# Attention: queries and keys without rotary part projected for two batches at once

## The reference, cut to what matters

```
q = x @ Wq.T ; k = x @ Wk.T ; v = x @ Wv.T
q_nope, k_nope: (B, 256, 16, 128)     q_rope, k_rope: (B, 256, 16, 64), rotated by position
scores = q_nope.k_nope / sqrt(128) + q_rope.k_rope / sqrt(64)
out = softmax(scores) . v ; x = layernorm(x + out @ Wo.T)
```

## Time and profile before

| | us |
|---|---|
| three runs | 673.15, 671.19, 672.73 (median 672.73) |
| the profiled execution | 671.22 |
| its span | 669.4 |
| the 16 slots of the first attention begin at | 22.06 |
| slot 15 begins at | 377.82 |

### The profile page before, as it was taken

The page is one execution under the profiler, slowest core; times in us unless marked ns, Lnnn a source line. Parts: engine busy times, 40 slices in busy tenths (PEclk is TensorE's granted clock), DMA queues, the critical chain, the costliest instruction groups (busy, mean ns, idle before and its releaser), DMA issues. The chain is left out here.

```text
span 669.4 us, 15275 instructions
## 1 busy us (share of the span) xinstructions
PE 656.9 (98%) x5297; PEld 632.3 (94%) x5297; DVE 439.2 (66%) x968; ACT 410.9 (61%) x1085; POOL 246.3 (37%) x279
## 2 busy tenths in 40 slices
PE   8999999999999999999999999999999999999995
PEld 8999999999999999999999899999997799999995
DVE  5566557656665765765675677556569986556877
ACT  5566667566776666766577773334689964333553
POOL 2731863034353133632329555112361462222011
PEclk9999999999999999999999999999999999999998
DMA  7174665435534445534363304100166100000010
GB/s 255 38 220 153 197 172 144 138 98 174 169 124 115 123 124 178 157 122 131 97 194 125 97 2 151 32 0 0 48 200 245 72 1 1 1 1 0 1 33 31
DMA packets 38172, 69.74 MB, mean 104 GB/s; under 512 B 3440, under 2 KB 22640, under 8 KB 37872
## 3 DMA queue, kind: packets, MB, share of 16 engines
q1 hardware_dynamic: 37696, 68.38, 33.6%
q10 hardware_dynamic: 432, 0.79, 0.4%
HBM read 52.18 MB, written 16.97 MB: 103 GB/s over the span
## 5 line engine op out<-in xcount | busy, mean ns | idle before, releaser
L312 PE MATMUL PJ<-xTh,WBh 128*128 128x256 f32 x364 | 106.7, 293 | 0.0
L314 PE MATMUL PJ<-xTh,WBl 128*128 128x256 f32 x364 | 103.0, 283 | 0.0
L313 PE MATMUL PJ<-xTl,WBh 128*128 128x256 f32 x364 | 102.8, 282 | 0.0
L851 POOL TENSOR_TENSOR stage<-stage 128x256 f32<-128x256 f32 x32 | 24.5, 766 | 162.8 <-DVE stage L718 162.8
L611 ACT ACTIVATE probs<-probs,rinv 128x256 f32<-128x256 f32 x128 | 58.4, 508 | 26.7 <-DVE rinv L734 26.7
L1229 PE MATMUL UG<-xTh,WBh 128*128 (+1 forms) x256 | 73.6, 288 | 0.3 <-PEq L54 0.3
L1232 PE MATMUL UG<-xTh,WBl 128*128 (+1 forms) x256 | 72.4, 283 | 0.0
L1230 PE MATMUL UG<-xTl,WBh 128*128 (+1 forms) x256 | 72.4, 283 | 0.0
L1301 ACT ACTIVATE ga<-UG 128x256 f32<-128x256 f32 x64 | 24.5, 383 | 75.5 <-PE UG L1232 75.5
L312 PEld LDWEIGHTS PJ<-xTh,WBh 128*128 128x128 f32 x364 | 69.6, 191 | 0.5
L313 PEld LDWEIGHTS PJ<-xTl,WBh 128*128 128x128 f32 x364 | 69.6, 191 | 0.0
(11 more groups left out here) (326 smaller groups left out, 2364.1 us busy)
## 6 DMA issues: line engine op xcount, KB each, us to landing
K<-scr_k SPq DMA_DIRECT2D x60, 256.0 KB, 4.4
raw<-in_w_att SPq DMA_DIRECT2D x37, 256.0 KB, 4.8
Q<-scr_q SPq DMA_DIRECT2D x15, 512.0 KB, 7.5
stage<-scr_m SPq DMA_DIRECT2D x6, 768.0 KB, 4.4
scr_q<-rot_h SPq DMA_DIRECT2D x30, 128.0 KB
scr_q<-rot_l SPq DMA_DIRECT2D x30, 128.0 KB
scr_k<-rot_h SPq DMA_DIRECT2D x30, 128.0 KB
scr_k<-rot_l SPq DMA_DIRECT2D x30, 128.0 KB
```

Of the source, the lines that this page charges most:

```text
L312: pe.matmul(out, ah, bh, start=(i == 0), stop=False)
L313: pe.matmul(out, ah, bl, start=False, stop=False)
L314: last = pe.matmul(out, al, bh, start=False, stop=(i == n - 1))
```

## The change

Queries and keys without rotary part are projected for a pair of batches: for slots 2 and 3, 4 and 5, and so on, one matmul streams 512 token columns. An odd slot computes heads 0 and 1 (weights at 2) of the next pair, an even slot heads 2 and 3 (weights at 4) of its own pair. `QKh[:, 0]` and `QKl[:, 0]` now hold heads 0 and 1 of both batches, `[:, 1]` heads 2 and 3. Slot 0 projects batch 1 in the old form, and so do the pieces ahead of the slots. The values stay as they were.

The rotary pieces stay in step 2 of even slots and go to step 0 of odd ones, where the other pieces go to steps 1 and 2. ACT takes the rotary parts one step later, as before: now step 1 of an odd slot. On POOL the splits of weights 8 and 9 go behind the rotations, and the split of the feed-forward weights waits for scores of slot 15. PSUM banks and waits follow the new order.

```diff
-        BANK = [1, 2, 0, 1, 2, 0, 0, 1]
+        FIRST_BANK = {2: 0, 3: 1, 4: 2, 6: 0, 7: 1}
+        PIECE_BANK = ([0, 1, 2, 0, 0, 1], [2, 0, 1, 2, 0, 1])
+        ROPE_BANK = ([1, 2], [0, 1])
...
-        ORDER = [([2], [3]), ([4], [5]), ([], []), ([6], [7])]
-        ROPE_STEP = 2
+        ROPE_STEP = (2, 0)
...
+        def pieces(k, j):
+            if k == 15 or j == ROPE_STEP[k % 2]:
+                return []
+            first = 2 * (j - 1) if k % 2 or j == 3 else 2 * j
+            return [first, first + 1]
+        def rope_now(k, j):
+            return k < 14 and j == ROPE_STEP[k % 2]
...
+            def project_two(out, at, col, b):
+                w, toks = slice(col * P, (col + 1) * P), slice(b * S, (b + 2) * S)
+                return three(out[:, :], [(WBh[:, at + t, w], WBl[:, at + t, w]) for t in range(KT)],
+                             [(xTh[:, t, toks], xTl[:, t, toks]) for t in range(KT)])
...
+            def piece(s, k, i):
+                n, out = 6 * (s + 1) + i, bank_of(k, i)
+                if k % 2 == 0:
+                    if i == 5 and k < 14:
+                        pe.wait_ge(rope_prod, 2 * s + 5)
+                    elif i < 5:
+                        pe.wait_ge(part_split, n - (1, 1, 4, 2, 0)[i])
...
+                    if k == 0 and i < 4:
+                        last = project(out, i + 2, slice(S, 2 * S))
+                    elif i < 4:
+                        last = project_two(out, 4, i, k % 4)
+                    else:
+                        last = project_values(out, TT * (k % 4 + 1) + i - 4)
                 else:
+                    if i < 3:
+                        pe.wait_ge(rope_prod, 2 * s + 4 + i)
+                    else:
+                        pe.wait_ge(part_split, n - 2)
...
+                    if i < 4:
+                        last = project_two(out, 2, i, (k + 1) % 4)
...
@@ ScalarE, emit
                     exps(u, j)
-                    if k < 15:
-                        for p in ORDER[j][0]:
-                            part(s + 1, k + 1, p)
-                    if j == ROPE_STEP + 1 and k < 14:
-                        part(s + 2, k + 2, 0)
+                    for i in pieces(k, j)[:1]:
+                        part(s, k, i)
+                    if j and rope_now(k, j - 1):
+                        rope_part(s + 2, k + 2, 0)
                     if k > 0 or j >= 1:
                         pT(u - 1, (j - 1) % 4)
                     normalise(u, j)
...
+                    for i in pieces(k, j)[1:]:
+                        part(s, k, i)
+                    if j and rope_now(k, j - 1):
+                        rope_part(s + 2, k + 2, 1)
                     if k > 0 or j >= 2:
                         oT(u - 2, k if j >= 2 else k - 1, (j - 2) % 4)
...
@@ VectorE, emit
-                    if j == ROPE_STEP and k < 14:
-                        part(s + 2, k + 2, 0)
+                    if rope_now(k, j):
+                        rope_part(s + 2, k + 2, 0)
+                    for i in pieces(k, j)[:1]:
+                        part(s, k, i)
...
@@ GpSimd, emit
-                if k == 5:
-                    for i in (8, 9):
-                        split_piece(GP * g + i, i)
...
                 if k < 14:
                     for p in range(2):
                         rotate(s + 2, k + 2, p)
+                if k == 5:
+                    for i in (8, 9):
+                        split_piece(GP * g + i, i)
...
             def split_down(q):
                 pool.wait_ge(tail_hi, q + 1)
+                pool.wait_ge(scores_ready, 4 * (SLOTS - 1) + q // 2 + 1)
```

More of the change, by code:

```diff
@@ L358, in rope_piece, with project_values @@
                 project(rope_bank(k, p), p, slice(b * S, b * S + S)).then_inc(rope_ready, 1)
[L360 to L371, removed]
+            def project_values(out, tile):
+                rows = slice(tile * P, (tile + 1) * P)
+                return three(out[:, :], [(xTh[:, t, rows], xTl[:, t, rows]) for t in range(KT)],
+                             [(WBh[:, 6 + t, :], WBl[:, 6 + t, :]) for t in range(KT)])
@@ L380, in piece @@
[L380 to L389, removed]
-                else:
-                    rows = slice(b * S + (p - 6) * P, b * S + (p - 5) * P)
-                    last = three(out[:, :], [(xTh[:, t, rows], xTl[:, t, rows]) for t in range(KT)],
-                                 [(WBh[:, 6 + t, :], WBl[:, 6 + t, :]) for t in range(KT)])
-                last.then_inc(piece_ready, 1)
+                    pe.wait_ge(part_split, 2)
@@ L396, in scores, with query, key @@
+            def query(part, k, j, rows):
+                if k < 2:
+                    return part[:, k, j, rows]
+                return part[:, j // 2, 2 * (j % 2), (k % 2) * S + rows.start:(k % 2) * S + rows.stop]
+            def key(part, k, j):
+                if k < 2:
+                    return part[:, k, j, S:2 * S]
+                return part[:, j // 2, 2 * (j % 2) + 1, (k % 2) * S:(k % 2 + 1) * S]
             def scores(s, k, j):
@@ L406, in scores @@
                 for t in range(TT):
-                    q, keys = slice(t * P, (t + 1) * P), slice(S, 2 * S)
+                    q = slice(t * P, (t + 1) * P)
                     out = bank[:, t, :]
                     both = t > 0 and not k
-                    pe.matmul(out, QKh[:, par, j, q], QKh[:, par, j, keys], start=not both, stop=False,
+                    pe.matmul(out, query(QKh, k, j, q), key(QKh, k, j), start=not both, stop=False,
                               skip_group_check=both)
-                    pe.matmul(out, QKh[:, par, j, q], QKl[:, par, j, keys], start=False, stop=False,
+                    pe.matmul(out, query(QKh, k, j, q), key(QKl, k, j), start=False, stop=False,
                               skip_group_check=both)
-                    pe.matmul(out, QKl[:, par, j, q], QKh[:, par, j, keys], start=False, stop=False,
+                    pe.matmul(out, query(QKl, k, j, q), key(QKh, k, j), start=False, stop=False,
                               skip_group_check=both)
@@ L531, in _ @@
             for p in range(2, 8):
-                piece(0, 0, p)
+                first_piece(p)
             for p in range(2):
@@ L589, in _, with rope_part, first_part, part @@
         def _(act):
[L590 to L599, removed]
+            def rope_part(s, k, p):
+                act.wait_ge(rope_sum, 4 * s + 2 * p + 2)
+                if k > 1:
+                    act.wait_ge(spill_k if p else spill_q, 64 * (s - 1))
+                act.activation(rot_dst(k, p, True), rope_f[:, 2 + p, :], ACT.Copy).then_inc(rope_hi, 1)
+            def first_part(p):
+                act.wait_ge(piece_ready, p - 1)
+                act.activation(first_dst(p, True), first_bank(p)[:, :], ACT.Copy).then_inc(part_hi, 1)
+            def part(s, k, i):
+                act.wait_ge(piece_ready, 6 * (s + 1) + i + 1)
+                act.activation(part_dst(k, i, True), bank_of(k, i)[:, :], ACT.Copy).then_inc(part_hi, 1)
             def exps(u, j):
@@ L707, in _, with rope_part, first_part, part @@
         def _(dve):
[L708 to L724, removed]
+            def rope_part(s, k, p):
+                dve.wait_ge(rope_ready, 2 * s + p + 1)
+                if k > 0 or p:
+                    dve.wait_ge(rope_sum, 4 * s + 2 * p)
+                if k == 0:
+                    dve.wait_ge(tab_in[p], 16)
+                bank = rope_bank(k, p)[:, :].rearrange("p (c n) -> p c n", c=2)
+                for f in range(2):
+                    table = tables[:, p, f:f + 1, :].broadcast_to([P, 2, S])
+                    last = dve.tensor_tensor(rope_f[:, f, :].rearrange("p (c n) -> p c n", c=2), bank, table,
+                                             ALU.mult)
+                last.then_inc(rope_prod, 1)
+            def first_part(p):
+                dve.wait_ge(part_hi, p - 1)
+                dve.tensor_tensor(first_dst(p, False), first_bank(p)[:, :], first_dst(p, True).bitcast(F32),
+                                  ALU.subtract).then_inc(part_split, 1)
+            def part(s, k, i):
+                dve.wait_ge(part_hi, 6 * (s + 1) + i + 1)
+                dve.tensor_tensor(part_dst(k, i, False), bank_of(k, i)[:, :], part_dst(k, i, True).bitcast(F32),
+                                  ALU.subtract).then_inc(part_split, 1)
             def row_max(u, j):
```

77 lines of the change are left out of this document (50 added, 27 removed).

## The result

The changed kernel takes 676.36 us (median of 14 runs, 673.98 to 683.95), the kernel before 671.40 beside it (median of 14, 670.41 to 673.42). The ratio is 1.0081, with a 95% interval of 1.0062 to 1.0100: slower by 0.8%. The profiled execution took 677.43 us, its span is 675.6.

What follows compares the result with a forecast made beforehand. PE was taken as the bound by its own matmul stream. Terms -2.8 + 0.2 + 3.3 + 3.1 = +3.8 us gave 675.0 or 676.5 by base; the middle, 675.8, was forecast, range 673.7 to 678.0.

Steps and rivals of the forecast that it cites:

- The fusion, -2.8: PE, slots 1 to 14: 336 matmuls of 512 columns replace 672 of 256, 2.8 us less, 0.2 us a slot.
- The 0.8 us by the Trainium skill: Fusion gain on PE by the page's formula N/2.4 + 2.5 ns alone: 336 x 2.5 ns; not used for the sum.
- The lower end of 2.4 us: Lower bound of the fusion's gain on PE, from the rounding of trace times; range 2.4 to 3.4 us.
- Slots 3, 7 and 11, +3.3: K lands 14.4 us into the slot, ACT waits 2.6 us, PE stands 1.1 us for values, three times.
- rival 2: Only slot 1 stands; in slots 3, 7 and 11 K lands some 1.1 us sooner: 672.5 us, chance 0.20.
- Slot 1, +3.1: ACT waits for late Q and K transfers, PE stands 3.8 us for values; less 0.7 at slot 2's fill, net 3.1.
- The saving of 0.7 at slot 2's fill: PE's existing wait for K's fill at slot 2, 0.7 us, is taken away by its later arrival.
- Slot 14, +0.2: PE already waits there 0.6 us; arriving 0.2 us earlier it waits 0.2 longer, so 0.2 of the gain is lost.
- DVE's slack elsewhere, 0: First step of odd slots: split of O ends later but keeps 0.55 us of slack; no cost, bound 0.3 us with POOL.
- 512-column operands: PE projections: operands and banks have the form of the 512-column matmuls shown, token for weight columns, so 0.232 us each.
- Rivals 4 and 1: 4: 512-column matmuls don't pay, 678.6 us, chance 0.12 with rival 3. 1: gain arrives whole, 669.4 us, chance 0.18.
- rival 3: Slow DVE operation in step 0 of odd slots uses up the slack: 678.8 us, chance 0.12 together with the 512-column rival.

Runs made afterwards that it cites:

- e1_unfused: The changed kernel with each 512-column piece issued again as matmuls of 256 columns, order and banks as in the change: 677.80 us, ratio 1.0085 to the kernel before.
- e5_act_later: The changed kernel with ACT taking its two rotary parts of odd slots in step 2 instead of step 1: 671.46 us, ratio 0.9993 to the kernel before.
- e9_dve14: The changed kernel with DVE splitting slot 14's key piece ahead of `OTl`, `rmax` and `nmax`: 674.76 us, ratio 1.0050 to the kernel before.
- e6_step2_dve14: The changed kernel with rotary pieces in step 2 of every slot and DVE's key-piece split earlier in slot 14: 669.91 us, ratio 0.9978 to the kernel before.
- e4_late: The changed kernel with two loads of 1 MB (`xres`, `w2t`) queued behind slot 0's spill: 677.57 us, ratio 1.0089 to the kernel before.
- e10_behind_fill: e6_step2_dve14 with both loads of 1 MB (`xres`, `w2t`) behind slot 0's fill for slot 2: 674.25 us, ratio 1.0050 to the kernel before.
- e2_step2: The changed kernel with the fusion kept but rotary pieces in step 2 of all slots, as before: 670.94 us, ratio 0.9987 to the kernel before.

## Why the prediction was right, and where only by its sum

675.8 was forecast, 676.36 came. The difference was forecast as +3.8 us and came as +5.0 by medians, +6.2 by the profiled executions; the forecast took 672.0 for the kernel before, which is 0.6 above its median and makes the two times look closer. The terms, by the profiles:

- **The fusion, -2.8.** Right: 0.232 us a matmul, 0.19 us a slot, -2.5 in slots 2 to 13, and e1_unfused loses just that. The 0.8 us by the Trainium skill ("TensorE: Matmul & The Clock Gate", Back-to-back issue gap) would have been wrong; the section gives that formula for isolated matmuls, not for a stream of weight load and matmul. The lower end of 2.4 us is an arithmetic slip: with 1.40 us for the six it is 80.6 - 78.4 = 2.2.
- **Slots 3, 7 and 11, +3.3.** This term failed in the profile. The mechanism is right: ACT waits for `scr_k<-rot_l` in all of them, and where K lands 14.3 us into the slot or later PE loses 0.9 to 1.35 us (1.1 forecast for 14.4). The landing was read off one execution as if it were a constant. It spreads from 12.9 to 14.6 us over those fifteen slots; in the profile after it was 13.2, 12.9 and 13.1, the term 0. That is rival 2's outcome, in this execution, though not for the reason given there: the spill is issued as early as before (0.97 us ahead of slot 7, before 0.95) and lands 13.9 us later instead of 15.3. What it was in the 14 timed ones is not known.
- **Slot 1, +3.1.** 3.8 us of waiting were forecast, steps 0 to 2 show 3.5 longer than an undisturbed odd slot's (19.02 against 15.49), 2.9 of it the one pause. The saving of 0.7 at slot 2's fill came true: PE starts slot 2 without a wait. The half clock took 1.5, and so the slot is 4.1 longer where 3.1 less 0.2 of the fusion was forecast. e5_act_later took the pause away without touching PE's order.
- **Slot 14, +0.2, the step that failed.** The prediction had "Pieces 0 and 1 of an even slot are wanted by scores two steps later, 2 and 3 too ... Those waits cost nothing while ACT and DVE keep pace", and then reckoned slot 14 by arrival alone. Slot 14 lost 3.1 us. Two steps are cover only if they hold work; its step 2 is two projections short, 2 x 12 x 0.120 = 2.9 us. Unfused, the waits there cost 1.6 us (e1_unfused, 23.66 against 22.06); the other 1.5, by difference, are the clock, which fell after three waits of 0.65 to 1.0 us. The DVE move alone saves 0.95 (e9_dve14), and without the moved rotary pieces it takes away the whole loss (e6_step2_dve14).
- **DVE's slack elsewhere, 0; 512-column operands.** Right: slots 5, 9 and 13 last 23.5 us, no wait for DVE there. Rivals 4 and 1 are out. So is rival 3 where it was looked for: a slow `nmax` of 1.28 us stands in step 0 of slots 3, 7 and 11 of the changed kernel, and PE loses nothing there. But its mechanism is at work in slot 14, with the 0.64 us shown above.
- **The clock.** In no term. 1.5 us in slot 1, 1.5 in slot 14 by difference, and 2.0 us in a later layer. That is 5.0 of the 6.2 us; waits, fusion and the rest leave 1.2.

From the forecast's +3.8 to the measured +6.2 it is -3.3 (slots 3, 7, 11), +3.1 (slot 14), +1.2 (slot 1), +2.0 (the later layer), -0.5 (up to slot 1, with unchanged work; unexplained) and -0.1 (fusion). So the total is near by luck: wrongs of both signs cancel. The direction was earned by the chain in slot 1 and by the late landings, both of which experiments confirmed; its size in this profile is mostly the clock's, which stood in no term of the forecast.

**The last 2.0 us** lie where nothing was changed. Around 524 us, in a layer after the attention, the change runs at 0.53 for 6 us (the last window above). The kernel before does the same work at 1.00 in its one profile. The two waits of PE ahead of the place, 0.22 and 0.29 us, stand in all twelve profiled executions, with and without the fall. Five of the twelve profiled executions have a slice below 0.9 at this place (the change, e4_late, e5_act_later, e9_dve14, e10_behind_fill), seven not, and the stretch from slot 15 on lasts 293.3 to 294.0 us in four of the five and 291.2 to 292.0 in the others; e4_late, whose dip is slight (0.82 over 6 us), has 291.8. Which edit brings it, or whether any does, stays open; it wasn't separated from the moment at which the stretch begins. The kernel before isn't free of such losses: of its 71 executions beside the experiments, 17 have a mean clock of 0.988 or 0.993 and a median of 673.4 us, the other 54 have 0.995 to 0.998 and 671.0. Where the clock fell in the 17 isn't on record. Open too is why K's transfer lands 13.8 to 15.8 us after the first issue of the spill in those fifteen slots. A second `rot_h`, which should take ACT's wait away, wasn't tried.

## What to carry to other kernels

Following each wait to its end paid; summing them by slot type didn't. When operations change places, check the odd one out (here the last slot, whose cover was missing) by hand: its distance in microseconds of work, not in steps. Take the time of a landing on which a stall hangs from several occurrences and executions, and put its spread into the range. Where a single-buffered tile makes an engine wait for a transfer, try first to place that wait later in the engine's own order: e5_act_later bought back 4.9 us so.

## What the runs showed of the hardware

- PE's granted clock went from 2.4 to 1.2 GHz after a pause of 2.9 us in slot 1, for some 3 us, which cost 1.5. In e1_unfused the same pause brought no fall. Three short waits in slot 14 (0.7, 0.65 and 1.0 us) were followed by one as well; in e1_unfused three much like them (0.5, 0.65 and 1.0) were not. A wait of 2.1 us at slot 2 was followed by one in e2_step2, one of 2.45 at the same place in e6_step2_dve14 wasn't. In the later layer a wait of 0.3 us was, in five of twelve executions. So the cost of a pause varies from one execution to the next, and a single profile shows one draw.
- 512-column matmuls of float32 pairs lie 0.232 us apart at full clock and 0.42 at half.
- The same spill landed 13.8 to 15.8 us after its first issue, and in e1_unfused, one program in one execution, at 14.1, 15.2 and 15.8.
- One DVE operation, `nmax` over 128x2, took 0.17 us in most places and 0.8 to 1.3 in some, at the same places in each round of the loop (1.28 in slots 3, 7 and 11 of the change). Why is open.
